# A retention stage re-laid in PSUM: states, turned keys, output and group sums in the banks of the heads' scores, statistics a slot later, normalising by ScalarE

## The reference, cut to what matters

```
qT, kT, vT = proj(Wq), proj(Wk), proj(Wv)        # 8 heads of 32
def step(S, qkv_t):
    S = g * S + k_t[..., :, None] * v_t[..., None, :]
    y_t = einsum('bhde,bhd->bhe', S, q_t)
out = ys.transpose(1, 0, 2, 3)
mean = out.mean(axis=(1, 3)); var = out.var(axis=(1, 3))   # over tokens and a head's channels
out = (out - mean) * rsqrt(var + EPS)
out = out.reshape(B, L, D) * gn_weight + gn_bias
x = layernorm(x + out @ Wo.T)
```

## Time and profile before

| | us |
|---|---|
| median of three runs (2560.79 to 2566.89) | 2562.2 |
| the profiled execution | 2562.65 |
| its span | 2560.8 |
| busy PE, DVE, ACT, POOL in the span | 2334.7, 1663.7, 1228.2, 725.9 |
| the profile's own share of PE on the chain that ended last | 70% |

### The profile page before, as it was taken

The page is one execution under the profiler, slowest core; times in us unless marked ns, Lnnn a source line. Parts: engine busy times, 40 slices in busy tenths (PEclk is TensorE's granted clock), DMA queues, the critical chain, the costliest instruction groups (busy, mean ns, idle before and its releaser), DMA issues.

```text
span 2560.8 us, 42694 instructions
## 1 busy us (share of the span) xinstructions
PE 2334.7 (91%) x16381; PEld 1379.9 (54%) x16432; DVE 1663.7 (65%) x4331; ACT 1228.2 (48%) x2774; POOL 725.9 (28%) x717
## 2 busy tenths in 40 slices
PE   5899999998789798886889999999999999999997
PEld 2333333333552476665556666666666666666664
DVE  5777777775530275665787667766777677776753
ACT  2655555555222251110566565566556655565540
POOL 2232223220110131111443333333333333333311
PEclk7999999999899899997999999999999999999999
DMA  8233333332219502000000000000000000000001
GB/s 293 90 108 97 108 102 99 110 118 79 90 68 412 245 2 87 22 18 36 1 5 5 5 3 4 5 5 30 3 12 30 28 13 18 5 22 22 19 21 37
DMA packets 70970, 158.59 MB, mean 62 GB/s; under 512 B 6336, under 2 KB 48432, under 8 KB 63184
## 3 DMA queue, kind: packets, MB, share of 16 engines
q1 hardware_dynamic: 68464, 146.68, 16.3%
q0 software_dynamic: 2304, 9.18, 1.6%
HBM read 116.52 MB, written 35.13 MB: 59 GB/s over the span
## 4 chain that ended last, share of the span: by engine, by line
PE 70%; DVE 16%; ACT 4%; DMA 4%; issue 2%; POOL 2%; SPq 1%; another core or an unknown queue 0%; POOLq 0%; DVEq 0%; ACTq 0%
PE banks L1846 9%; PE banks L1824 6%; PE banks L1705 6%; PE banks L245 4%; PE banks L1719 4%; PE banks L213 4%; PE banks L221 3%; PE banks L1806 3%; PE banks L1325 3%; PE banks L1749 2%; PE banks L284 2%; PE banks L265 2%; PE banks L1764 2%; DVE arena L2355 2%; DMA arena<-in_e_Wg 2%
## 5 line engine op out<-in xcount | busy, mean ns | idle before, releaser
L439 DVE TENSOR_REDUCE arena<-banks 128x1 f32<-128x512 f32 x512 | 323.8, 682 | 113.1 <-PE banks L213 113.0
L354 ACT ACTIVATE arena<-banks 128x512 f32<-128x512 f32 x512 | 279.4, 595 | 165.6 <-PE banks L221 144.1
L1846 PE MATMUL banks<-arena 128*128 128x512 f32 x640 | 293.2, 594 | 6.3 <-DVE arena L2063 5.9
L1916 ACT ACTIVATE arena<-arena 128x256 f32<-128x256 f32 (+1 forms) x512 | 286.3, 562 | 3.4 <-DVE arena L2016 3.1
L2154 POOL TENSOR_TENSOR arena<-arena 128x512 f32<-128x512 f32 x128 | 162.8, 1272 | 401.3 <-DVE arena L2047 401.2
L1705 PE MATMUL banks<-arena 128*128 128x512 f32 x512 | 245.4, 602 | 5.7 <-DVE arena L2047 4.9
L213 PE MATMUL banks<-arena 96*128 96x512 bf16 x512 | 203.8, 400 | 20.5 <-DVE arena L439 12.4
L2150 POOL TENSOR_TENSOR arena<-arena 128x16 f32<-128x16 f32 x64 | 187.5, 2930 | 5.3
L1846 PEld LDWEIGHTS banks<-arena 128*128 128x128 f32 x640 | 116.5, 190 | 131.8 <-issue 119.6
L221 PE MATMUL banks<-arena 128*128 128x512 bf16 x461 | 175.6, 384 | 3.3 <-ACT arena L354 1.8
L1888 ACT ACTIVATE arena<-arena 128x256 f32<-128x256 f32 (+1 forms) x256 | 102.1, 471 | 154.4 <-DVE arena L1992 154.4
(11 more groups left out here) (302 smaller groups left out, 4421.4 us busy)
## 6 DMA issues: line engine op xcount, KB each, us to landing
arena<-in_e_W SPq DMA_DIRECT2D x32, 1024.0 KB, 12.1
arena<-stacks SPq DMA_DIRECT2D x64, 384.0 KB, 4.5
arena<-in_e_Wg SPq DMA_DIRECT2D x16, 1024.0 KB, 14.5
stacks<-arena SPq DMA_DIRECT2D x32, 384.0 KB, 2.5
stacks<-arena SPq DMA_DIRECT2D x32, 256.0 KB, 2.7
arena<-dens POOLq DMA_DIRECT2D x32, 256.0 KB, 4.5
arena<-in_xT SPq DMA_DIRECT2D x8, 512.0 KB, 9.0
stacks<-arena SPq DMA_DIRECT2D x32, 128.0 KB, 2.5
```

The source lines that it names most:

```text
L354: e.activation(ex[:, j], self.psum[:, 3 + k % 2], ACT.Exp).then_inc(s["a_e"], 1)
L439: e.tensor_reduce(mx[:, t, j:j + 1], self.psum[:, k % 3], AX.X, ALU.max, negate=True).then_inc(s["a_m"], 1)
L1846: i = e.matmul(bank, weights[:, c], self.hT[:, c], start=c == 0, stop=c == 1)
L1916: k = e.activation(pr[:, h, at:], pr[:, h, at:], ACT.Exp, bias=mx[:, h:h + 1], scale=rn[:, h:h + 1], accum_out=den[:, h:h + 1])
```

## The change

What stays in the ring of banks 0 and 1 is q, k, values and the turning. States and keys go to banks 2 and 3, the group sums of both groups together to columns 0 to 3 of bank 2, the output to banks 4 and 5. Those are the banks of the own scores, so new waits order them: states wait for the masks of own scores of group 0 (r_a), own scores of group 1 for the states' masks (r_mask), keys for the masks of group 1, own scores of group 0 for keys' copies (r_kn), the means (r_mean) and the residual add (r_x) of the slot before. The order on PE in a slot becomes q group 0, own scores group 0, q group 1, states, k, y group 0, own scores group 1, values, y group 1, keys, turning, output first half, group sums, output second half. The layer norm's statistics move to the head of the next slot on DVE, its reciprocal root (now with -mean times root beside it, two more POOL instructions) and its applying, now four ACT instructions, follow there, all for sequence n-3. The group norm's yn is made by ACT as well, from coefficients that DVE forms for both groups at once. The other lines of the diff rename semaphores and join the two groups' small tiles.

```diff
         uses = []
         for n in range(SLOTS3):
-            a, b, c, d = n < SEQS, 0 <= n - 1 < SEQS, 0 <= n - 2 < SEQS, 0 <= n - 3
-            uses += [("q", n, 0), ("q", n, 1)] * a + [("st", n - 1, 0), ("st", n - 1, 1)] * b + [("turn0", n - 3, 0), ("turn1", n - 3, 0)] * d
-            uses += [("k", n, 0), ("k", n, 1), ("nat", n, 0), ("nat", n, 1), ("kt", n, 0), ("kt", n, 1)] * a
-            uses += [("wo", n - 2, 0), ("wo", n - 2, 1)] * c + [("stat", n - 1, 0), ("stat", n - 1, 1)] * b
+            uses += [("q", n, 0), ("q", n, 1), ("k", n, 0), ("k", n, 1), ("nat", n, 0), ("nat", n, 1)] * (n < SEQS)
+            uses += [("turn0", n - 3, 0), ("turn1", n - 3, 0)] * (0 <= n - 3)
...
         if a is not None:
             self.tensor3_project(e, w, "q", a, 0)
+        if b is not None:
+            self.tensor3_own(e, w, b, 0)
+        if a is not None:
             self.tensor3_project(e, w, "q", a, 1)
         if b is not None:
             self.tensor3_state(e, w, b, 0)
             self.tensor3_state(e, w, b, 1)
-            self.tensor3_own(e, w, b, 0)
-        if n >= 3:
-            self.tensor3_turn(e, w, n - 3)
...
             self.tensor3_y(e, w, b, 1)
+            w.wait_ge("r_a", 8 * b + 8)
         if a is not None:
             self.tensor3_keys(e, w, a, 0)
             self.tensor3_keys(e, w, a, 1)
-        if 0 <= n - 2 < SEQS:
-            self.tensor3_out(e, w, n - 2, 0)
-            self.tensor3_out(e, w, n - 2, 1)
+        if d is not None:
+            self.tensor3_turn(e, w, d)
+        if c is not None:
+            self.tensor3_out(e, w, c, 0)
         if b is not None:
-            self.tensor3_stat(e, w, b, 0)
-            self.tensor3_stat(e, w, b, 1)
+            self.tensor3_stat(e, w, b)
+        if c is not None:
+            self.tensor3_out(e, w, c, 1)
...
         w.wait_ge("r_kn", 2 * b + g + 1)
         w.wait_ge("r_vn", 2 * b + 2)
-        bank = self.bank3(w, "st", b, g)
+        w.wait_ge("r_a", 8 * b + 4)
+        bank = self.psum[:, 2 + g]
...
+        elif g == 0:
+            w.wait_ge("r_kn", 2 * b + 2)
+            w.wait_ge("r_mean", b)
+            if b >= 2:
+                w.wait_ge("r_x", 2 * (b - 1))
         else:
-            w.wait_ge("r_a", 8 * b + 4 * g)
+            w.wait_ge("r_a", 8 * b + 4)
+            w.wait_ge("r_mask", 2 * b + 2)
...
+        a, c, d = (k if 0 <= k < SEQS else None for k in (n, n - 2, n - 3))
+        if d is not None:
+            small, x = self.norm3[d % 2], self.x_nat[:, d]
+            w.wait_ge("r_rstd", d + 1)
+            for t in range(TILES):
+                i = e.activation(x[:, t], x[:, t], ACT.Identity, scale=small[:, 32 + t:33 + t], bias=small[:, 44 + t:45 + t])
+            i.then_inc(self.s["r_norm"], 1)
+        if c is not None:
+            for g in range(2):
+                w.wait_ge("r_coef", c + 1)
+                if c >= 2:
+                    w.wait_ge("r_wo", 2 * (c - 1))
+                e.activation(self.yn3[c % 2][:, g], self.psum[:, 6 + g], ACT.Identity, scale=self.st3[:, g, 14:15], bias=self.st3[:, g, 16:17]).then_inc(self.s["r_yn"], 1)
...
+        if d is not None:
+            self.stats_of(e, w, "r_x", [2 * d + 1, 2 * d + 1, 2 * d + 2, 2 * d + 2], self.norm3[d % 2], self.x_nat[:, d], self.s["r_sn"])
         if a is not None:
             self.vector3_decay(e, w, "q", a, 0)
+        if b is not None:
+            self.vector3_own(e, w, b, 0)
+        if a is not None:
             self.vector3_decay(e, w, "q", a, 1)
-        if c is not None:
-            self.vector3_normed(e, w, c, 0)
-            self.vector3_normed(e, w, c, 1)
         if b is not None:
             self.vector3_state(e, w, b, 0)
             self.vector3_state(e, w, b, 1)
-            self.vector3_own(e, w, b, 0)
+        if c is not None:
+            self.vector3_coefficients(e, w, c)
...
-            self.stats_of(e, w, "r_x", [2 * c + 1, 2 * c + 1, 2 * c + 2, 2 * c + 2], self.norm3[c % 2], self.x_nat[:, c], self.s["r_sn"])
-        if b is not None:
-            self.vector3_mean(e, w, b, 0)
-            self.vector3_mean(e, w, b, 1)
-        if c is not None:
-            w.wait_ge("r_rstd", c + 1)
-            self.normalise(e, self.norm3[c % 2], self.x_nat[:, c], self.s["r_norm"])
```

More of the change, by code:

```diff
@@ L1260, in layout3 @@
         few = Columns(self.arena, self.R + 8224, self.R + 8224 + 512)
-        self.st3 = [few.take(32) for _ in range(2)]
+        self.st3 = split(few.take(64), 2, 32)
         self.norm3 = [few.take(64) for _ in range(2)]
@@ L1386, in tensor3_y, with tensor3_stat @@
         i.then_inc(self.s["r_y"], 1)
[L1388 to L1391, removed]
+    def tensor3_stat(self, e, w, b):
+        w.wait_ge("r_sq", 2 * b + 2)
+        if b + 1 < SEQS:
+            w.wait_ge("r_kn", 2 * (b + 1) + 1)
+        for g in range(2):
+            i = e.matmul(self.psum[:, 2, 2 * g:2 * g + 2], self.S("same_head32"), self.st3[:, g, 6:8], start=True, stop=True)
+        i.then_inc(self.s["r_stat"], 1)
     def tensor3_out(self, e, w, b, pair):
-        yn = self.yn3[b % 2]
+        yn, bank = self.yn3[b % 2], self.psum[:, 4 + pair]
         w.wait_ge("r_yn", 2 * b + 2)
-        bank = self.bank3(w, "wo", b, pair)
         for t in range(2):
@@ L1427, in scalar3_slot @@
+        if a is not None:
+            if a >= 2:
+                w.wait_ge("r_y", 2 * (a - 1))
             for pair in range(2):
-                w.wait_ge("r_nat", 2 * n + pair + 1)
-                e.activation(self.vn3[n % 2][:, 2 * pair:2 * pair + 2], split(self.psum[:, self.ring3.bank(("nat", n, pair))], 2, CH), ACT.Copy).then_inc(self.s["r_vn"], 1)
+                w.wait_ge("r_nat", 2 * a + pair + 1)
+                e.activation(self.vn3[a % 2][:, 2 * pair:2 * pair + 2], split(self.psum[:, self.ring3.bank(("nat", a, pair))], 2, CH), ACT.Copy).then_inc(self.s["r_vn"], 1)
@@ L1430, in scalar3_slot @@
             for g in range(2):
-                w.wait_ge("r_kt", 2 * n + g + 1)
-                e.activation(self.kn3[n % 2][:, :, g * P:(g + 1) * P], split(self.psum[:, self.ring3.bank(("kt", n, g))], TILES, P), ACT.Copy).then_inc(self.s["r_kn"], 1)
+                w.wait_ge("r_kt", 2 * a + g + 1)
+                e.activation(self.kn3[a % 2][:, :, g * P:(g + 1) * P], split(self.psum[:, 2 + g], TILES, P), ACT.Copy).then_inc(self.s["r_kn"], 1)
+        if d is not None:
+            for k, done in enumerate(("r_xTb", "r_xTa")):
+                w.wait_ge("r_put%d" % k, d + 1)
+                e.activation(self.xT[:, d, k, 1:], self.psum[:, self.ring3.bank(("turn%d" % k, d, 0))], ACT.Copy).then_inc(self.s[done], 1)
@@ L1462, in vector3_slot @@
                 w.wait_ge("r_wo", 2 * c + pair + 1)
[L1463 to L1470 removed]
+                e.tensor_tensor(x, x, split(self.psum[:, 4 + pair], 2, CH), ALU.add).then_inc(self.s["r_x"], 1)
     def vector3_decay(self, e, w, kind, b, g):
@@ L1493, in vector3_sums @@
     def vector3_sums(self, e, w, b, g):
-        own, st = self.own1, self.st3[g]
+        own, st = self.own1, self.st3[:, g]
         w.wait_ge("r_y", 2 * b + g + 1)
@@ L1515, in vector3_normed, with vector3_coefficients @@
+    def vector3_coefficients(self, e, w, b):
+        own, st, S = self.own1, self.st3, self.S
+        w.wait_ge("r_rs", b + 1)
+        if b:
+            w.wait_ge("r_yn", 2 * b)
+        e.tensor_tensor(st[:, :, 14], st[:, :, 12], S("r_gw"), ALU.mult).then_inc(own.up(), 1)
         w.wait_ge(own.sem, own.n)
-        e.tensor_tensor(st[:, 15:16], st[:, 8:9], st[:, 14:15], ALU.mult).then_inc(own.up(), 1)
+        e.tensor_tensor(st[:, :, 15], st[:, :, 8], st[:, :, 14], ALU.mult).then_inc(own.up(), 1)
@@ L1517, in vector3_normed @@
         w.wait_ge(own.sem, own.n)
[L1518 to L1522, removed]
-    def gpsimd3(self, e, w):
-        for n in range(1, SLOTS3 - 1):
-            b, c = n - 1, n - 2
+        e.tensor_tensor(st[:, :, 16], S("r_gb"), st[:, :, 15], ALU.subtract).then_inc(self.s["r_coef"], 1)
@@ new lines, in gpsimd3 @@
+    def gpsimd3(self, e, w):
+        own = self.ownp1
+        for n in range(1, SLOTS3):
+            b, d = n - 1, n - 3
+            if d >= 0:
+                small = self.norm3[d % 2]
+                w.wait_ge("r_sn", d + 1)
+                e.tensor_scalar(small[:, 40:44], split(small[:, 24:32], TILES, 2)[:, :, 0], -1.0, None, ALU.mult).then_inc(own.up(), 1)
+                self.rsqrt(e, w, small, own.sem)
+                own.up()
+                w.wait_ge(own.sem, own.n)
+                e.tensor_tensor(small[:, 44:48], small[:, 40:44], small[:, 32:36], ALU.mult).then_inc(self.s["r_rstd"], 1)
@@ L1544, in gpsimd3_state, with gpsimd3_rsqrt @@
         e.tensor_tensor(s3[:, 2], s3[:, 2], s3[:, 1], ALU.add).then_inc(self.s["r_cum"], 1)
[L1546 to L1549, removed]
+    def gpsimd3_rsqrt(self, e, w, b):
+        own, st = self.ownp1, self.st3
+        w.wait_ge("r_var", b + 1)
+        e.tensor_scalar(st[:, :, 13], st[:, :, 11], EPS, None, ALU.add).then_inc(own.up(), 1)
```

(2 more changed lines are left out.)

51 lines of the change are left out of this document (17 added, 34 removed).

## The result

The changed kernel takes 2536.18 us (median of four runs, 2531.89 to 2539.71) against 2563.22 us for the kernel before in the same sessions: a ratio of 0.9893 with a 95% interval of 0.9873 to 0.9912, 27 us faster. The forecast was 2539 us, range 2529 to 2552.

What follows compares the result with a forecast made beforehand. PE's work was taken to bound each slot, with 3.71 us of waits on top. Slot terms put the next stage's start at 1191.3 instead of 1214.56; 2562.65 - 23.3 - 0.45 = 2538.9, given as 2539 us, range 2529 to 2552.

Steps and rivals of the forecast that it cites:

- PE is the floor and its waits are the price: Retention slots: PE's work sets the floor, 24.51 of 28.32 us, and its waits of 3.71 us make up the rest.
- The old waits: PE's waits before q, turning, k and output and between group sums all go, 3.7 us a slot.
- PE's work 23.8 and the new wait 1.25, slot 25.1: Slots 3 to 7: 23.8 us of PE work plus 1.25 waiting for own-score masks before states, say 25.1.
- Yn's slack: Group norm on ACT: y of group 0 has 1.6 us in hand before it would wait; the thinnest cover.
- Normalising on ACT hides: Layer norm's applying on ACT, 2.06 us, ends at 6.9 us; turning is at 18.8, so 12 us over.
- The lower clock goes: Full slots: q's part at the lower clock, 1.7 us in three slots, goes; q runs at its 3.4 us rate everywhere.
- the clock still falls: Rival, chance 0.20: lower clock costs 1.7 us in three to six slots, slot 8 at half; 2548 to 2553 us.
- yn late: Rival, chance 0.12: y of group 0 waits 1 to 2 us for ACT in six slots; 2545 to 2551 us.
- the clock down behind the new wait: Rival, chance 0.03: the wait before the states lowers the clock, 10.0 us of work doubles in six slots; 2599 us.
- Slot 8: Slot with only own scores, states, y, turning, output: 25.1 us taken, 20.6 at full clock, 29 with half rate after states.
- The sum: Retention stage: next stage's first matmul moves from 1214.56 to 1191.3 us, 23.3 us gained, all of it kept.
- The rule against it: DVE's coefficients beside POOL's state additions: charged nothing, though the skill's lockout rule would make them up to 1.4 us late.

Runs made afterwards that it cites:

- The added wait: Changed kernel with PE's projection of q made to wait for the layer norm's statistics in slots 3 to 7; 2551.77 us, 0.9960 of before.
- The run with k first: Changed kernel with the first half of k put before the states on PE and DVE; 2538.67 us, 0.9903 of before.
- repeat: Changed kernel measured once more, unaltered; 2537.63 us, 0.9901 of before.
- The fastest version above: Changed kernel with the first half of k before the states and yn's coefficients directly behind the masks of own scores on DVE; 2529.02 us, 0.9872 of before.
- the kernel before's repeat: Kernel before the change measured once more, unaltered; 2560.14 us in one run.

## Why the prediction was right, step by step

*PE is the floor and its waits are the price.* Right. The added wait shows it directly, 2.73 us of slot for 2.51 of waiting.

*The old waits.* Right as a sum (3.7 us, all gone), wrong if read one by one: taking the 1.33 us before q alone brought 2.27 us elsewhere. The banks without the later statistics gave 27.32 us slots; the later statistics without the banks were not run, so that the gain needs both is shown for one side only.

*PE's work 23.8 and the new wait 1.25, slot 25.1.* Slot 24.43. The prediction had PE reach the states at 4.61 us; it got there at 4.90 (the three pieces start 1.82, 1.10 and, with its end, 1.99 us apart), and the masks ended at 5.6 instead of 5.7, since they follow the decay of q without a gap (first mask at 3.12). So the wait was 0.74, below the 0.9 that "it can't be below": the mis-sized term. PE's work was 23.69, not 23.8. Five slots make 3.3 us of the difference.

*Slot 2* 23.8 predicted, 23.6 measured.

*Yn's slack.* 1.6 us predicted, 1.0 measured: yn0 takes 0.77 on the mean and not 0.6, and the coefficients were 0.37 us longer. The run with k first used it up, which shows it was rightly called the thinnest cover.

*Normalising on ACT hides.* Right (2.07 us, no one waits in full slots); that it isn't needed in full slots wasn't said.

*The lower clock goes.* The forecast had all full slots at the full clock, and it was so in both executions of the changed kernel. But the prediction did not derive it: it weighed waits behind which the clock had fallen against waits behind which it had not, and the runs show that their length doesn't decide (see below). These 5.1 us of the 25.0 came in partly by luck. The rival that the clock still falls (0.20), yn late (0.12), the clock down behind the new wait (0.03) did not come true.

*Slot 8* 25.1 predicted; 26.8 and 23.9 in the two executions, inside the 20.6 to 29 given. Inside it a term was mis-sized: y of group 0 was to begin at 8.1 us and began at 9.75, since the states ran partly at half rate (2.50 us) and DVE's masks and coefficients and ACT's yn follow them one by one. *Slot 9* 14.0 predicted, 14.2 and 13.7; *slot 10* 9.6, 9.6. *Slot 1* was to stay the same and took 21.9 and 21.5 us for 21.1 and 21.0 before.

*The sum.* 23.3 us predicted for the stage, 25.0 and (repeat against the kernel before) 28.4 measured. The next stage gave back 1.1 us in the one and 4.0 in the other pair (from its first matmul to the end of the span 1346.2 before, 1347.4 and 1350.2 after; the kernel before's repeat 1346.2). The prediction kept "all of it". The fastest version above shows 1346.1 there and the kernel before with its means first 1350.4, in code that all have alike, so it is not shown to be a cost of the change.

*The rule against it.* The prediction trusted the 0.16 us rows inside POOL's 1.04 us instruction and said these rows speak against the Trainium skill, SBUF — State Buffer, section Who interferes with whom. That step failed. The second coefficient instruction ends at 1071.23, POOL's addition beside it at 1071.22; the third at 1071.64, the next addition at 1071.63; with POOL idle both take 0.16. So here a two-input instruction on DVE does wait for POOL's read of SBUF, as the page states, in slots 2 to 7 of both executions. The rows that seemed to say otherwise were read beside POOL's power on four columns; there the trace departs from the page. The wait cost 0.37 us of yn's slack and no time in a full slot, and 0.3 us in slot 8.

## What to carry to other kernels

When a few banks go round as a ring through engines with long queues, a single wait's length need not be what its removal brings: the wait can go to the next user of the ring, as it did here. Follow what stands ahead of the releasing instruction on its own engine; here statistics, reciprocal root and normalising ahead of a decay cost 2.9 us a slot (27.32 against 24.43, banks and PE's order alike), and moving them a slot later brought that, while giving the normalisings to another engine brought nothing in a full slot. Then look for the wait that is left, and fill it with work whose inputs are ready, but check the next thinnest cover in the same step: k before the states alone gave 0.2 us a slot, with the coefficients early 1.0.

## What the runs showed of the hardware

The granted clock fell in three of five full slots of the kernel before, in both profiles, at the start of q, behind 0.76 and 1.33 us of waiting with only two matmuls of 2 columns between them (0.94 in the mean of a slot of 30.0 us, 1.00 in one of 28.3). With the 1.33 us gone it fell again in three of five, at the states, behind 2.27 to 2.29 us in one piece. It fell in none of the five slots with 2.51 us waited in one piece before q and 0.69 before the states, and in one of five (slot 3, which lasted 28.9 us) with 3.62 us in one piece before the states. So the length of PE's idle time alone does not tell when the clock falls, and the 5.1 us of the gain that came from it could not be foreseen by a count of idle microseconds. What does tell stays open.

POOL's power on 128x4, 1.04 us long, left a two-input instruction of DVE that began 0.31 us into it at its 0.16 us, while POOL's addition on 128x128 held such instructions until it ended (0.31 and 0.38 us, and 0.45 in slot 8). The instructions beside the power were 128x1 and those beside the addition 128x2, so that POOL's operation decides is likely and not shown.
